# Moving an expert tile's y store behind the hi parts of act and of the next tile on ScalarE

## The reference

```python
x = x + moe(cond(x, weight, adapter_ids), ...)      # x: 8 x 256 x 1024, float32
cond:   einsum('bsi,boi->bso', x, weight[adapter_ids])
moe:    probs  = softmax(h @ gate_w.T)              # 16 experts, the best 2 for each token
        g, u   = split(h @ w_gate_up[e].T)          # 2 x 256 columns for each expert
        out_e  = (silu(g) * u) @ w_down[e].T        # back to 1024 columns
        result = sum over the two experts of weight * out_e  +  the shared expert (1024 inner columns)
```

## Time and profile before

| | |
|---|---|
| median of 3 runs | 1063.91 us (1063.42 to 1065.25) |
| the profiled execution | 1064.86 us, of which 1063.1 us is the span from the first to the last instruction |
| granted TensorE clock | 1.000 of full speed over the whole span |
| TensorE busy | 1055.3 us, 99% of the span |
| VectorE, ScalarE, GpSimd busy | 60%, 43%, 26% of the span |

### The profile page before, as it was taken

The page is one execution under the profiler, slowest core; times in us unless marked ns, Lnnn a source line. Parts: engine busy times, 40 slices in busy tenths (PEclk is TensorE's granted clock), DMA queues, the critical chain, the costliest instruction groups (busy, mean ns, idle before and its releaser), DMA issues.

```text
span 1063.1 us, 15851 instructions
## 1 busy us (share of the span) xinstructions
PE 1055.3 (99%) x4826; PEld 870.8 (82%) x4827; DVE 634.1 (60%) x650; ACT 457.0 (43%) x527; POOL 272.8 (26%) x325
## 2 busy tenths in 40 slices
PE   8999999999999999999999999999999999999998
PEld 7888888888888888887888888888888888888887
DVE  6666765536756667867866867354553545544454
ACT  6565644532223556756655755232223222322310
POOL 1000000000026655555555550121003200033040
PEclk9999999999999999999999999999999999999999
DMA  9899877422256779987987865663566336564355
GB/s 351 325 348 342 315 286 258 190 79 81 88 209 211 263 273 348 335 313 270 352 351 265 291 248 213 246 229 119 145 232 237 138 118 182 194 237 144 113 183 211
DMA packets 55350, 248.03 MB, mean 233 GB/s; under 512 B 8146, under 2 KB 21586, under 8 KB 45394
## 3 DMA queue, kind: packets, MB, share of 16 engines
q1 hardware_dynamic: 29394, 161.50, 42.0%
q0 software_dynamic: 19008, 62.41, 17.0%
q10 hardware_dynamic: 6912, 23.66, 5.9%
HBM read 200.87 MB, written 43.52 MB: 230 GB/s over the span
## 4 chain that ended last, share of the span: by engine, by line
PE 98%; DMA 1%; issue 1%; DVE 0%; ACT 0%; SPq 0%; ACTq 0%; DVEq 0%
PE bank L568 32%; PE bank L570 32%; PE bank L569 32%; PE bank L593 1%; PE bank L779 1%; DMA raw<-cond_w 0%; ACT w_split_sb L863 0%; PE bank L581 0%; PE bank L712 0%; PE bank L602 0%; DVE w_split_sb L1157 0%; DMA ids<-ids 0%; PE bank L699 0%; PE bank L747 0%; DVE rows L1413 0%
## 5 line engine op out<-in xcount | busy, mean ns | idle before, releaser
L1157 DVE TENSOR_TENSOR w_split_sb<-raw,w_split_sb 128x2048 fp32r<-128x2048 f32 (+3 forms) x152 | 257.3, 1724 | 60.0 <-ACT w_split_sb L863 58.8
L863 ACT ACTIVATE w_split_sb<-raw 128x2048 fp32r<-128x2048 f32 (+3 forms) x152 | 215.7, 1456 | 63.7 <-PE bank L570 53.5
L507 POOL DMA_INDIRECT h_in<-h_dram,idx_h x156 | 175.5, 1125 | 122.6 <-DVE tile_f L1462 75.1
L568 PE MATMUL bank<-hT_hi,w_split_sb 128*128 128x512 f32 x512 | 199.7, 390 | 0.0
L569 PE MATMUL bank<-hT_lo,w_split_sb 128*128 128x512 f32 x512 | 199.2, 389 | 0.0
L570 PE MATMUL bank<-hT_hi,w_split_sb 128*128 128x512 f32 x512 | 199.2, 389 | 0.0
L568 PE MATMUL bank<-w_split_sb,tile_hT 128*128 (+1 forms) x312 | 124.8, 400 | 0.0
L570 PE MATMUL bank<-w_split_sb,tile_hT 128*128 (+1 forms) x312 | 122.0, 391 | 0.0
L569 PE MATMUL bank<-w_split_sb,tile_hT 128*128 (+1 forms) x312 | 121.7, 390 | 0.0
L570 PEld LDWEIGHTS bank<-hT_hi,w_split_sb 128*128 128x128 f32 x512 | 96.1, 188 | 20.0
L568 PEld LDWEIGHTS bank<-hT_hi,w_split_sb 128*128 128x128 f32 x512 | 96.1, 188 | 19.9
(11 more groups left out here) (153 smaller groups left out, 1417.0 us busy)
## 6 DMA issues: line engine op xcount, KB each, us to landing
raw<-sh_gu_w SPq DMA_DIRECT2D x16, 2048.0 KB, 9.3
raw<-exp_gu_w SPq DMA_DIRECT2D x16, 2048.0 KB
raw<-cond_w SPq DMA_DIRECT2D x14, 2048.0 KB, 9.8
y_dram<-y_out ACTq DMA_DIRECT2D x39, 512.0 KB
raw<-sh_down_w SPq DMA_DIRECT2D x8, 2048.0 KB, 7.7
raw<-exp_down_w SPq DMA_DIRECT2D x16, 1024.0 KB
h_dram<-h_blk POOLq DMA_DIRECT2D x16, 512.0 KB, 8.8
x_raw_sb<-xT SPq DMA_DIRECT2D x7, 1024.0 KB, 9.6
```

The costliest lines, as they stand in the source:

```text
L507: nc.gpsimd.indirect_dma_start(out=h_in[par][:, i, :], out_offset=None, in_=h_blocks, in_offset=bass.IndirectOffsetOnAxis(ap=idx_h[par][:, ...
L568: nc.tensor.matmul(dst, lhs[0], rhs[0], start=first, stop=False)
L863: return nc.scalar.activation(dst, src, ACT.Copy)
L1157: return nc.vector.tensor_tensor(dst, src, hi.bitcast(F32), ALU.subtract)
```

## The change

`y_send` is called later in ScalarE's step: behind `act_hi` and `tile_hi` instead of right behind `y_evict`. With it go its own wait for `y_ev` and the DMA that it issues. The waits of `act_hi` and `tile_hi` (for TensorE's transpose, for `gu_mm`, and for the turned rows) now stand ahead of the store. Nothing else moves; in the last step, which has no `tile_hi`, the store stands behind `act_hi`.

```diff
                 if y_count is not None:
                     y_evict(s - 2, par, y_count)
-                    y_send(s - 2, par)
                 act_hi(s - 1, 1 - par)
                 act.wait_ge(gu_mm, s + 2)
                 if not last:
                     tile_hi(s + 1, 1 - par, tile_hT[1 - par])
+                if y_count is not None:
+                    y_send(s - 2, par)
                 if last:
                     act.wait_ge(raw_in[0], 16 * (POST // 2 + 1))
```

## The result

The changed kernel takes 1066.04 us (median of 17 runs, 1064.23 to 1069.38) against 1063.94 us for the kernel before (17 runs, 1063.05 to 1065.82). The ratio is 1.0023 with a 95% interval of 1.0016 to 1.0029: slower by 2.1 us, about the 0.2% that the prediction gave as the least that can be told from no change; a ratio of 1 lies outside the interval. The times are also wider apart: 5.2 us from lowest to highest, against 2.8 before.

The account below looks back on a forecast made before the run. The prediction took TensorE, busy 99% of the span, to bound the kernel. Its three terms, 0 + 0 - 0.4 us, applied to the median of 1063.91 us, gave 1063.5 us, with a range of 1062.8 to 1065.3 us.

Parts of the forecast that it names:

- the second rival: Gate and up loads: displaced stores delay them; three late loads give 1066.3 us, five 1067.9 us; chance 0.05.
- What bounds the kernel: Expert stage: TensorE, busy 99% of the span, sets the time and loses only about 0.97 us in 38 steps.
- First part: ScalarE's act_hi and tile_hi lose the send ahead of them; act_hi up to 0.42 us earlier in few steps; priced 0.
- Second part: ScalarE's weight copies or silu get the send ahead of them, 0 to 0.63 us a step, covered; priced 0.
- The cover: e_act's lead on TensorE's transpose, 2.24 us, at least 1.40 us in another step with a store; exceeds the send's 0.63 us.
- Third part: The store's DMA is issued 1.5 to 2.9 us later, freeing step 16's late weight load; gain 0 to 0.7, taken 0.4 us.
- Rival 1: Whole kernel: no change at all, not even in step 16's stall; 1063.9 us; counted within the forecast's 0.90.
- Rival 3: ScalarE: the send in front of silu eats e_act's lead; 0.2 us in 15 steps would give 1066.9 us; chance 0.02.
- Rival 4: Expert stage: act_hi ahead of the send shortens steps, to no less than 1062.9 us; over 0.2% faster by something unseen, 0.03.

Follow-up runs that it names:

- late_load_steps: Against the kernel before, the store is moved late only in steps that issue the next gate and up load: 1066.47 us against 1064.20, ratio 1.0016.
- the small stores: Changed kernel with each store sending 16 of 128 rows and the last stage gathering from weights instead: 1063.96 us, ratio 0.9996; same edits on kernel before: 1063.99 us.
- send_before_silu: Against the kernel before, the store's send is moved to just ahead of silu: 1066.26 us against 1064.03, ratio 1.0026.

## Why the prediction was wrong

The forecast was 1063.5 us in a range of 1062.8 to 1065.3, with 0.90 on no change. The measured 1066.04 us is outside. The outcome was the second rival, to which I gave 0.05.

**What bounds the kernel: right.** TensorE sets the time, and the stage before lost 0.97 us of 319.77.

**First part, act_hi earlier, priced at 0: right, as far as is seen.** It waits for the transpose in 38 steps now, and the late store in the other steps measured 1.0000.

**Second part, the send ahead of silu and the weight copies: the price of 0 was right, its working was not.** I took 0.46 to 0.63 us for the cost of a send from a place where it stood behind y_evict and waited for `y_ev`. Behind tile_hi it is issued while the copy runs and costs ScalarE nothing (414.01 against a copy from 413.97 to 415.02). That also puts the issue 0.7 us behind the transpose and not 1.8 us, as I had it for step 16. The cover was also not what I took it for: I left e_act's lead as it was, and late loads brought it down to 0.67 us.

**Third part, the DMA's later issue: this is the step that failed.** I priced it at -0.4 us from one store, that of step 16, which stands at the end of a load. The runs showed +2.1 us in its place. That moving the store of step 16 helps is not shown: in the trace after, ScalarE still waited 1.69 us for the same load instead of 2.91. I had written of the store of step 15 that it moves by 1.5 us, and drew no consequence. That one stands ahead of a load. In the sentence "the store's bytes were in the same traffic before" I treated the traffic as one pool. It wasn't: before, those bytes went mostly between the end of the loads before and the first packet of the next one, which came 0.96 to 2.24 us behind its issue: in 11 of the 13 load steps the store's last packet had started by then. In step 15 the engines moved nothing at all around the store's issue at 464.72 (two windows of the trace before; the last two numbers are the DMA share and GB/s):

```profile
...
463.00:464.00 1.00, 1.00 (x6) 0.84 (x5) 1.00 (x2) 0.91 (x3) 0.24 (x1) 1.00 0.00 0
464.00:465.00 1.00, 1.00 (x7) 0.81 (x6) 1.00 (x2) 0.55 (x2) 0.91 (x1) 1.00 0.00 0
...
```

The load issued 0.66 us behind that store, at 465.38, is the very one that came late before. Its store was the closest ahead of a load of all 13, so the late load that I read as the fault of step 16's store may have been step 15's; no run separates the two. In the 5.4 us of the earlier trace rows the store of 471.67 moved nothing until 475.4 and its 0.21 MB behind that, so its 9.6% is not a share held over the whole time, as I read it.

Moved by 1.5 us (in step 9 from 0.79 us ahead of the transpose to 0.74 us behind), these bytes fall into the load's time, and it arrives up to about 1 us later. ScalarE had taken up the weights without idle time in nearly all steps, but with little to spare, so that 1 us more became six waits. The trace before could have shown it: the traffic by queue in one load step would have been enough.

A second term of this part was wrong without showing in the median. I held y_evict safe because a store lands within 12.2 us and y_evict comes 16.8 us later. After the change y_evict comes as early as 12.9 us behind the issue of the store that it waits for, and one store took 13.2 us to land: y_evict waited 1.5 us for it. No wait of TensorE is traced to that.

**The size.** I priced a late load at 0.80 us and asked for three to pass 0.2%. In the trace after, the late loads cost TensorE no wait for e_act; what they do is take its lead away. The next load is issued later too, as its buffer comes free later (steps 11, 13 and 15 above), so the lateness is carried from expert to expert. In late_load_steps the lead was used up at three transposes. A further disturbance, such as a gather that lands late, then has less cover, and a wait of TensorE near 2 us was followed by 3.4 us at half clock. That this is why the loss differs between 0 and 5 us from run to run is likely and not shown, since only one execution of each kernel is profiled. How much of the median's 2.1 us is the late load alone, and how much the gathers that meet it, stays open: the profiled execution is near the top of its range, and its largest loss began with a gather. Its gather's own lateness isn't explained: GpSimd was idle for 6.95 us between two of its four issues, with no cause shown, and the trace before has such a gap at the same place (4.86 us, ended at 588.20) with no harm. That giving the load more time removes most of the loss is shown, and so is that the store's place in load steps alone brings it.

**The rivals.** Rival 1 (no change) is what happens when the store is late only in steps without a load. Rival 2 is the outcome; its threshold was of the right order, its chance far too low, and I held against it that the store moves away from the end of loads, which says nothing of the stores ahead of a load. Rival 3 fell with the small stores. Rival 4 (faster) found no sign in any run. The rule of DMA: Bandwidth & Descriptors (the Trainium skill, "Queues, rings and completion order"), that each engine takes turns between queues, pointed the right way. The traces agree with it in one thing: in send_before_silu, from 419.82 us, the store's queue and SyncE's were both served in the same 5 us (22.3% and 57.6% of the engines' time). They don't show turns from the issue on: there the store had none in the first 4 us behind its own issue, and in the first window after, the store had 59.6% and the load, issued 0.24 us later, had none. Whether the load had work on the engines by then is not shown; in the 13 load steps of this trace its first packet came no sooner than 0.92 us behind its issue.

## What to carry to other kernels

Where a load has just enough time, ask what stands ahead of its issue on the DMA engines: a store that ran in the idle stretch before it was free here, and some 1.5 us later the same store cost 2.1 us in all. Look at the traffic by queue around the issue of the tightest load, and look at each kind of step by itself, since one move can help one kind and hurt the other. The lead of each operand is a reserve against the spread of DMA times; spending it can leave most steps untouched and still lengthen the runs.

## What the runs showed of the hardware

- After TensorE had been idle for 1.9 us, the granted clock fell from full speed to 0.5 about 1.25 us after it had started again (607.26 us), and stayed there for 3.4 us; matmuls went from 0.23 to 0.43 us apart.
- A DMA issued on ScalarE's queue while a copy of 1.05 us runs doesn't hold up the next copy; the same send behind its own wait for a copy's end kept the engine for 0.46 us (464.72 to 465.18 before).
- How soon a store's first packet came differed with its place beside the load: one issued 0.36 to 0.69 us behind a load of 2 MB had its first packet 4.1 to 4.3 us behind its issue (five steps of send_before_silu), one issued 0.04 to 0.25 us ahead of the load 0.9 to 1.0 us behind its issue (five steps of the trace after).
- With stores of 64 KB instead of 512 KB the kernel of before is not measurably faster (0.9997, 0.9988 to 1.0006), although some 18 MB of stores (39 x 448 KB) are gone: at this place in time their volume costs nothing that can be seen, while the late place of the full stores costs 2.1 us.
